# A graph network of four layers: where the last dense bias is added to the residual rows

## What is computed

```
h = relu(gat_conv(x, W1, b1))            # 512 -> 1024
h = relu(gat_conv(h, W2, b2))            # 1024 -> 1024
x = layernorm(x + h @ Wfc + bfc)         # 1024 -> 512
```

## Time and profile before

| | |
|---|---|
| Three timed runs | 2528.84, 2535.97, 2541.94 us; median 2535.97 |
| The profiled execution's own time | 2555.53 us |
| Its span, first to last instruction | 2553.5 us |
| Mean granted TensorE clock | 0.952 of 2.4 GHz |
| GpSimd's bias adds (line 2303) | 40 |
| DMA | 394.21 MB, mean 154 GB/s |

### The profile page before, as it was taken

One profiled execution on the slowest core, in us unless ns is written; L12 is line 12 of the kernel. 1 busy time (PEld: TensorE's weight loads), 2 busy tenths in 40 slices (PEclk: granted clock), 3 DMA queues, 4 the chain that ended last, 5 costly groups with the idle time before them and its releaser, 6 DMA issues.

```text
span 2553.5 us, 33436 instructions
## 1 busy us (share of the span) xinstructions
PE 2341.6 (92%) x10787; PEld 1879.7 (74%) x10787; DVE 1527.5 (60%) x4649; ACT 996.9 (39%) x2005; POOL 1020.3 (40%) x971
## 2 busy tenths in 40 slices
PE   6977699968999999899989999999998988989997
PEld 5855488856888888777768888888876766767775
DVE  6745377743666854333326664588776775767654
ACT  5942012211256632121214664334335544545343
POOL 2042606627032234345532222157664545542532
PEclk8987799988999999999989999999999989999998
DMA  5423155552267732222225665566665646554432
GB/s 181 142 98 105 47 187 184 178 158 62 77 216 250 255 125 92 73 70 92 77 65 178 238 232 181 165 212 215 205 207 186 210 165 196 191 175 159 151 109 68
DMA packets 171539, 394.21 MB, mean 154 GB/s; under 512 B 44967, under 2 KB 73902, under 8 KB 170830
## 3 DMA queue, kind: packets, MB, share of 16 engines
q0 software_dynamic: 65296, 184.67, 23.1%
q1 hardware_dynamic: 106090, 207.66, 23.1%
HBM read 221.98 MB, written 170.25 MB: 154 GB/s over the span
## 4 chain that ended last, share of the span: by engine, by line
PE 63%; DVE 6%; issue 5%; ACT 2%; DMA 1%; POOL 0%; another core or an unknown queue 0%; DVEq 0%; ACTq 0%; POOLq 0%
PE g_h_ps L2443 12%; PE g_h_ps L2445 12%; PE g_h_ps L2444 12%; PE g_t_ps L2424 5%; PE g_h_ps L2468 4%; PE g_h_ps L2470 4%; PE g_h_ps L2469 4%; PE g_h_ps L1715 1%; PE g_h_ps L1713 1%; PE g_h_ps L1714 1%; DVE g_x_hi L2693 1%; PE g_sum_ps L965 1%; PE g_sum_ps L966 1%; PE g_misc_ps L1457 1%; PE g_h_ps L1725 1%
## 5 line engine op out<-in xcount | busy, mean ns | idle before, releaser
L2443 PE MATMUL g_h_ps<-held_w_hi,g_x_hi 128*128 128x512 f32 x1264 | 519.3, 411 | 14.6 <-issue 11.8
L2445 PE MATMUL g_h_ps<-held_w_hi,g_x_lo 128*128 128x512 f32 x1264 | 502.1, 397 | 13.5 <-issue 13.3
L2444 PE MATMUL g_h_ps<-held_w_lo,g_x_hi 128*128 128x512 f32 x1264 | 501.0, 396 | 13.3 <-issue 13.0
L2545 ACT ACTIVATE g_act_t<-g_t_ps,g_b_col 128x256 f32<-128x256 f32 (+1 forms) x640 | 264.2, 467 | 482.8 <-PE g_t_ps L2424 352.4
L2693 DVE CAST g_x_hi<-g_act_t 128x512 fp32r<-128x512 f32 (+1 forms) x320 | 151.1, 472 | 299.3 <-ACT g_act_t L2545 240.5
L594 DVE CUSTOM_DVE_ANT_0 g_prod<-g_h_sb,g_a_rows 128x256 f32<-128x256 f32 x632 | 224.7, 422 | 169.4 <-ACT g_h_sb L492 143.9
L2445 PEld LDWEIGHTS g_h_ps<-held_w_hi,g_x_lo 128*128 128x128 f32 x1264 | 241.5, 191 | 71.2 <-issue 18.4
L2443 PEld LDWEIGHTS g_h_ps<-held_w_hi,g_x_hi 128*128 128x128 f32 x1264 | 241.7, 191 | 63.9 <-issue 17.3
L423 PE MATMUL g_h_ps<-g_w_hi,g_x_hi 128*128 128x512 f32 x616 | 247.7, 402 | 44.5 <-issue 19.2
L2444 PEld LDWEIGHTS g_h_ps<-held_w_lo,g_x_hi 128*128 128x128 f32 x1264 | 242.2, 192 | 61.8 <-issue 18.3
L2468 PE MATMUL g_h_ps<-fc_w_hi,g_x_hi 128*128 128x512 f32 x632 | 280.7, 444 | 1.2 <-DVE g_x_lo L2695 0.7
(11 more groups left out here) (386 smaller groups left out, 4134.9 us busy)
## 6 DMA issues: line engine op xcount, KB each, us to landing
h<-g_h_sb SPq DMA_DIRECT2D x158, 512.0 KB
g_x_in<-h SPq DMA_DIRECT2D x59, 512.0 KB
g_x_in<-in_dram SPq DMA_DIRECT2D x40, 512.0 KB
h<-g_rows_own SPq DMA_DIRECT2D x40, 512.0 KB
x<-fc_x SPq DMA_DIRECT2D x20, 512.0 KB
x<-conv_x SPq DMA_DIRECT2D x20, 512.0 KB
g_w_raw<-in_dram SPq DMA_DIRECT2D x12, 512.0 KB, 4.8
fc_w_raw<-in_dram SPq DMA_DIRECT2D x20, 256.0 KB
```

Source lines behind the costliest of these rows:

```text
L2443: pe.matmul(out, xh, wh, start=(k == 0), stop=False)
L2444: pe.matmul(out, xh, wl, start=False, stop=False)
L2445: last = pe.matmul(out, xl, wh, start=False, stop=(k == KC - 1))
L2545: last = act.activation(act_t[:, k, 0:width], t_ps[f % 2][:, c, 0:width], ACT.Relu, bias=b_col[:, m // GM, k:k + 1])
```

## The change

The bias is added once, ahead of time, to all rows of `x`, and the sum is kept in a new table `xb` in DRAM. Twenty groups of four tiles (the last has three) pass through two buffers of SBUF memory that the edge sums of the first attention layer have just left (`rows_src`, `rows_own`). SyncE loads group g at half step 53 + 2g and stores it three half steps later; VectorE adds the bias two tiles at a time, after that half step's attention. Later the gathers of the residual read `xb`, GpSimd's add is gone, and VectorE's `add_rows` waits for the gather itself. GpSimd waits for the last store at h = 101, before the second layer's edge work uses the memory, and again at the first gather. The loads share the semaphores `fc_in` with those of `Wfc`, whose thresholds rise.

```diff
@@
 
 
 def node_layers(nc, sem, held, h1, al1, scan_row, row_d, row_s, map_d, map_s, slot_tab, b1, avec, h2, al2, bounce1, bounce2,
-                wfc, b2, x_rows, b_out, x1_out, y_out, conv_w, x2_rows, u_tab, w_in, w_o1s, w_o1v, w_o2s, w_o2v, x3_rows,
+                wfc, b2, x_rows, b_out, xb_rows, x1_out, y_out, conv_w, x2_rows, u_tab, w_in, w_o1s, w_o1v, w_o2s, w_o2v, x3_rows,
                 mlp_w_t, mlp_b):
 
     KC = HC // P
@@
     src_ahead = {-4: 0, -3: 1, -1: 2, 0: 3, **{paced(t) + 1: t + 4 for t in range(ET - 4)}}
     own_ahead = {paced(t) - 1: t for t in range(ET)}
     WFC = SUMS2 + SPAN + 2
+    XB, XB_TILES = SUMS1 + SPAN + 3, 4
+    XB_GROUPS = -(-TILES // XB_TILES)
+    assert XB + 2 * XB_GROUPS + 3 < 2 * D_DONE + 1
     LN_STEPS = 7
     X1_MACROS = ENDS // 2
 
@@
         e.fwd = Space(nc, "g2", fwd_at)("fwd", [H, EP])[:, :]
         e.h_src = [rows_src[:, s * HC:(s + 1) * HC] for s in range(2)]
         e.own = [rows_own[:, s * HC:(s + 1) * HC] for s in range(RING)]
+        early = Space(nc, "xb", rows_at)
+        xb = [early(f"rows{s}", [P, XB_TILES, D]) for s in range(2)]
+        assert early.end <= fwd_at
         e.tabs = tabs
         small_at = sb.end
         e.al_src = sb("al_src", [P, ET, 2 * H])
@@
         fc_hi_done = sem("fc_w_hi_done")
         fc_lo_done = sem("fc_w_lo_done")
         res_in = [sem(f"fc_res_in{s}") for s in range(2)]
-        res_done = sem("fc_res_done")
+        xb_done = sem("xb_done")
+        xb_stored = sem("xb_stored")
         summed = sem("fc_summed")
         ln = sem("fc_ln")
         logged = sem("fc_logged")
@@
 
         def by_pool(m):
             return m < GM or any(A_TILES <= t < ENDS for t in tiles(m))
+
+        def xb_tiles(g):
+            return range(XB_TILES * g, min(XB_TILES * (g + 1), TILES))
 
         def with_x1(m):
             return tiles(m)[0] < ENDS
@@
 
                         sp.wait_ge(fc_lo_done, k - 1)
                     sp.dma_start(fc_raw[:, k % 2, :], wfc[k * P:(k + 1) * P, :]).then_inc(fc_in[k % 2], 16)
+
+                def rows_of(table, g):
+                    t = xb_tiles(g)
+                    return table[t[0] * P:(t[-1] + 1) * P, :].rearrange("(j p) k -> p j k", p=P)
+
+                def load_xb(g):
+                    if g == 0:
+                        sp.wait_ge(signals.finished, e1.past(ET, ET))
+                        for q in range(RING):
+                            sp.wait_ge(signals.stored[q], e1.all_stored(q))
+                    if g >= 2:
+
+                        sp.wait_ge(xb_stored, 16 * (g - 1))
+                    sp.dma_start(xb[g % 2][:, 0:len(xb_tiles(g)), :], rows_of(x_rows, g)).then_inc(fc_in[g % 2], 16)
+
+                def store_xb(g):
+                    sp.wait_ge(xb_done, g + 1)
+                    sp.dma_start(rows_of(xb_rows, g), xb[g % 2][:, 0:len(xb_tiles(g)), :]).then_inc(xb_stored, 16)
 
                 def load_rows(m):
                     s = m % 2
@@
                         e1.load_row(sp, at1[h - 1] + 4)
                     if h % 2 == 1 and 0 <= (h - 3) // 2 < TILES:
                         store((h - 3) // 2)
+                    if h - XB in range(0, 2 * XB_GROUPS, 2):
+                        load_xb((h - XB) // 2)
+                    if h - XB in range(3, 2 * XB_GROUPS + 3, 2):
+                        store_xb((h - XB) // 2 - 1)
                     if WFC <= h < WFC + KC:
                         load_fc(h - WFC)
                     if h == first_half[m] and m + 2 < MACROS and not by_pool(m + 2):
@@
                     s = m % 2
                     if m == GM:
                         pool.wait_ge(al_done, 8 * len(WITH_EDGES))
+                        pool.wait_ge(xb_stored, 16 * XB_GROUPS)
                     if m >= GM + 2:
 
                         pool.wait_ge(summed, fc_done(m - 2))
                     for j, t in enumerate(tiles(m)):
-                        pool.indirect_dma_start(x_res[s][:, j, :], None, x_rows, at(t, NODE)).then_inc(res_in[s], 16)
-
-                def add_bias(m):
-                    s, n = m % 2, len(tiles(m))
-                    pool.wait_ge(res_in[s], res_landed(m))
-                    pool.tensor_tensor(x_res[s][:, 0:n, :], x_res[s][:, 0:n, :], b_rows[:, 0:n, :],
-                                       ALU.add).then_inc(res_done, 1)
+                        pool.indirect_dma_start(x_res[s][:, j, :], None, xb_rows, at(t, NODE)).then_inc(res_in[s], 16)
 
                 def scatter_y(m):
                     s = m % 2
@@
                         if 0 <= n < 4 * ET:
                             look_map(n)
                     if h == 2 * D_DONE + 1:
+                        pool.wait_ge(xb_stored, 16 * XB_GROUPS)
                         for q in range(RING):
                             pool.wait_ge(signals.stored[q], e1.all_stored(q))
                         pool.wait_ge(signals.summed, e1.past(ET, ET))
@@
                     if h == SCORE2 + 6:
                         pool.wait_ge(side_done, 1)
                     edge_gathers(e2, SUMS2, h)
-                    if h == GH - 2:
-                        pool.wait_ge(b_rows_in, 32)
                     if h + 1 < HALVES and halves_of[h + 1][0] >= GM and h + 1 == first_half[halves_of[h + 1][0]]:
                         gather_res(halves_of[h + 1][0])
-                    if m >= GM and h == first_half[m]:
-                        add_bias(m)
                     if m - 2 >= GM and h == first_half[m]:
                         scatter_y(m - 2)
                     if h >= GH:
@@
                         e.share_sums(act, t)
 
                 def round_fc(k):
-                    act.wait_ge(fc_in[k % 2], 16 * (k // 2 + 1))
+                    act.wait_ge(fc_in[k % 2], 16 * (XB_GROUPS // 2 + k // 2 + 1))
                     if k == 0:
                         for q in range(RING):
                             act.wait_ge(signals.stored[q], e2.all_stored(q))
@@
                 def add_rows(h):
                     m, j, _ = halves_of[h]
                     s = m % 2
-                    dve.wait_ge(res_done, m - GM + 1)
+                    dve.wait_ge(res_in[s], res_landed(m))
                     if m >= GM + 2 and with_x1(m - 2):
 
                         dve.wait_ge(x1_done, m - GM - 1)
@@
                     if g == FIRST_PAIR:
                         mlp.split_pair(dve, 0)
 
+                def add_bias(g):
+                    if g == 0:
+                        dve.wait_ge(b_rows_in, 32)
+                    dve.wait_ge(fc_in[g % 2], 16 * (g // 2 + 1))
+                    n = len(xb_tiles(g))
+                    for j in range(0, n, 2):
+                        part = xb[g % 2][:, j:min(j + 2, n), :]
+                        last = dve.tensor_tensor(part, part, b_rows[:, 0:min(2, n - j), :], ALU.add)
+                    last.then_inc(xb_done, 1)
+
                 for h in range(GH):
                     m = halves_of[h][0]
                     before(e1, SCORE1, h)
@@
                         split(m + 1, f)
                     if h // 2 in WITH_EDGES:
                         attention(h)
+                    if h - XB in range(2, 2 * XB_GROUPS + 2, 2):
+                        add_bias((h - XB) // 2 - 1)
                     after(e1, SUMS1, at1, h)
                     after(e2, SUMS2, at2, h)
                 for u in range(TILES):
@@
     x1 = table("x1", [ENDS * P, D])
     x2, x3 = table("x2", [2 * EP, D]), table("x3", [2 * EP, D])
     u_tab = table("u_tab", [EP, 256])
+    xb = table("xb", [NP, D])
     def stage(build, *args):
 
         held = []
@@
     stage(dense_and_prep, x_t, w1, a1, h1, al1, ends_row, ends_col, ew_col, rec_d, rec_s, scan_row, row_d, row_s, map_d, map_s,
           perm_tab, slot_tab, attr20_t, pw1, pb1, pw2b, attr4_col, u_tab, w2, held)
     stage(node_layers, held, h1, al1, scan_row, row_d, row_s, map_d, map_s, slot_tab, b1, a2, h2, al2, bounce1, bounce2,
-          wfc, b2, x, bfc, x1, out, conv_w, x2, u_tab, w_in, w_o1s, w_o1v, w_o2s, w_o2v, x3, mlp_w_t, mlp_b)
+          wfc, b2, x, bfc, xb, x1, out, conv_w, x2, u_tab, w_in, w_o1s, w_o1v, w_o2s, w_o2v, x3, mlp_w_t, mlp_b)
 
 
 def kernel(**inputs):
```

## The result

The changed kernel takes 2515.52 us (median of 5, 2508.12 to 2521.89) against 2534.86 (median of 5, 2522.16 to 2541.94) on the same chip: ratio 0.9937, 95% interval 0.9909 to 0.9965. The forecast was 2521.0 against 2535.97, a ratio of 0.9941. The number is right; much of the reason is not, and that is what the rest is about.

What follows compares the result with a forecast made beforehand. Time can be won only where TensorE idles and its clock is below 1. Holds of 8.7 us plus 6.5 us of clock, added work at 0, give 15.2 us or 0.6% off 2535.97: 2521 us, range 2506 to 2549.

Steps and rivals of the forecast that it cites:

- Gain so far: 8.7 + 6.5 = 15.2 us.: Dense step: 8.7 us of VectorE holds come off four TensorE waits, and 6.5 us of slow clock after three come back.
- all of it can come off TensorE: Dense step: each of four waits is longer than the VectorE hold before it, so the holds' 8.7 us all come off.
- rival 1: Dense step: the next engine takes the regained time, only the two long casts' 5.4 us come off; 2531 us, chance 0.18.
- Below nothing I see no way: VectorE and SP only get more to do.: Look-up stretch, 1054 to 1190: the added work and traffic cannot make it faster; cost taken as 0.
- the batch's hold (+27.4 us at most, 0 at least): Look-ups: twelve-look-up batches delay ScalarE's eviction; new traffic costs 0, or 27.4 us if TensorE's idle and clock losses double.
- The rule on descriptor generation: Look-ups: VectorE adds reading two SBUF operands would not lengthen GpSimd's batches, as descriptor generation needs the write interface instead.
- 17 us as the price if it was false: Look-ups: if VectorE's adds do slow descriptor generation, some 14 adds in seven batches could lengthen them by 17 us.
- 41.4 MB at no cost: Second layer, some 930 to 1190: loading and storing 79 tiles raises traffic to 258 and 232 GB/s; cost 0.
- VectorE's 48 us at no cost: Second layer, some 930 to 1190: VectorE's 40 adds of 1.21 us fit its idle time; cost 0, up to 48 without slack.
- Rival 2: Look-ups, 1054 to 1190: row traffic delays the batches, holding ScalarE's eviction longer; +12 us net, 2548 us, chance 0.21.

Runs made afterwards that it cites:

- e1: Kernel before with GpSimd's 40 bias adds taken out and nothing in their place (result lacks the last bias): 2527.64 us, ratio 0.998.
- e2: Changed kernel with its pass over the rows kept but the result unused, and GpSimd's 40 adds back: 2513.65 us, 0.9922 of the kernel before.
- e7: Kernel before, GpSimd's adds kept, plus VectorE's 40 adds on scratch rows at the changed kernel's places, no loads or stores: 2514.5 us, ratio 0.9949.
- e14: Kernel before without GpSimd's adds (bias left out), look-ups paced to the half step TensorE is at, no VectorE pass: 2521.04 us, ratio 0.991.
- e3: Changed kernel without VectorE's 40 adds, rows loaded and stored unchanged (bias left out): 2535.57 us, 1.0007 of the kernel before.
- e5: Kernel before with the bias added per pair in the dense step by VectorE instead of GpSimd, no pass: 2531.58 us, ratio 1.0002.
- e11: Kernel before with look-ups paced to the half step TensorE is at, on another chip: 2403.85 us, ratio 1.0003.
- e13: Kernel before with six look-ups per half step instead of three, on the chip where the kernel before takes 2403.99 us: 2415.89 us, ratio 1.0055.

## Why the prediction was right, and where it was not

The sum came out, 0.9941 forecast and 0.9937 measured, because two errors cancelled on the slower chips: the dense step brought less than forecast, and the look-ups brought what the forecast did not have. That the number fits is luck.

- **"Gain so far: 8.7 + 6.5 = 15.2 us."** The place and the chain are right: without the adds conv is 5.4 to 8.8 us shorter (178.4 to 175.0 against 183.8), and every run with the adds, or with VectorE's own in their place, has 182.5 to 184.1. On the other chip both terms are there nearly at size, 6.2 and 5.8. On the slower chips they are smaller: in the changed kernel's conv, idle time fell by 2.5 us and the matmuls took 3.3 less. And by the traces, single ones with some scatter, most of that comes back behind conv, in part at the wait for painn_msg; the total gets about 5 us (e1). The step that was wrong is "all of it can come off TensorE": each hold was charged in full to one wait, as if no other wait stood ready. This is rival 1, which had priced the whole gain at 5.4 us.
- **"Below nothing I see no way: VectorE and SP only get more to do."** This is the step that failed outright. In the look-ups TensorE's idle time went from 16.8 to 4.5 us. e2, e7 and e14 show some 11 to 20 us there and behind: A is 685.1, 687.6 and 683.0 us against 698.4 to 703.4 in the runs that have neither adds nor waits beside the look-ups (e1, e3, e5). I had priced the batch's hold (+27.4 us at most, 0 at least) as something that could only grow. The row that I quoted, an eviction that comes when the batch ends while few bytes move, already suggested that bytes don't hold it; the next question, what would shorten it, I did not ask.
- **The rule on descriptor generation.** Beside the two-input adds a look-up takes up to 1.98 us, in the run with the one-input instruction 1.20 at most, without either 1.21. So the inference in the Trainium skill, SBUF — State Buffer, Who interferes with whom, that such a VectorE instruction leaves descriptor generation alone, does not hold here. I had worked out 17 us as the price if it was false. Here it does not hold, and the sign of the price was wrong: a batch became some 1.8 us longer, and the stretch shorter.
- **41.4 MB at no cost**: borne out where the price was put. e3 moves them beside the look-ups (224 GB/s) and idles as e1 does. For the whole kernel it is open (e3 and e1 are 7.9 us apart).
- **VectorE's 48 us at no cost**: right in size, 40 adds of up to 1.22 us, VectorE busy 46.5 us with them; TensorE has no wait for x_lo there.
- **Rival 2** (batches hold longer) had the right place and the wrong direction: evictions and relus together waited 182.5 us with a DMA as releaser before and 126.5 after.

Left open: what holds ScalarE during a batch, and why VectorE's adds end it. In the kernel before, evictions begin at 1092.93 and 1098.38; TensorE's matmuls go on without a gap, so the next was due near 1103.8, and it came at 1109.53. The profile names a DMA as releaser, with tensor names that have nothing to do with the wait. Spreading the batch removes the hold, the adds shorten it, and one chip does not show it. That it grows with the row of DMAs is read from traces; no run changed that length alone where the hold exists. The first stage, too, differs by chip: TensorE is busy 152.83 of the 200 us from 100 to 300 in the kernel before on a slower chip, and 193.44 in e11.

## What to carry to other kernels

When a forecast has an unexplained stall next to new work, bound it on both sides: a change can shorten it as well as lengthen it. When time comes off one wait, look for the next wait of the same engine before you count it. Ask for each part of a change alone: here the part that was meant to cost nothing brought the gain, and a run with its result unused (e2) showed that in one step. A wait that spreads a batch must still let its last piece out on time; look at the next thing on that queue before placing it.

## What the runs showed of the hardware

- On the slower chips, while GpSimd issues 10 to 20 small gathers in a row (0.95 us each, 0.30 between), ScalarE can stand for 7.6 to 17.8 us without taking up the half step that TensorE has finished; the wait is longer behind a longer row, and behind rows of 8 there was none over 3 us. On another chip a row of 90 held nothing (e13).
- On the slower chips a pair of VectorE's two-input adds of 128x1024 in the batch cuts that wait: ten waits of 3.8 to 4.5 us ended 0 to 0.8 us behind such a pair.
- A VectorE tensor_tensor of 128x1024 with both inputs and the output in SBUF delays GpSimd's gather beside it from 0.95 to as much as 1.98 us; a tensor_reduce over the same elements does not (0.95 to 0.96 for look-ups that lie wholly beside one). Another gather, for the edges, shows it in the changed kernel's order of time, 3.94 us beside two instructions on 4x2561 elements:

```profile
1214.92 2.81 DVE L1022 TENSOR_TENSOR g_cut<-g_keys 4x2561 f32<-4x2561 f32 x1
1215.43 3.94 POOL L897 DMA_INDIRECT g_al_src<-al,held_tabs  x1 [0.30 <-issue]
1217.76 1.49 DVE L1024 TENSOR_SCALAR g_cut<-g_cut 4x2561 f32<-4x2561 f32 x1
```

- The kernel before takes 2404 us on one chip and 2529 to 2545 on the others, so only ratios on one chip were compared.
